# SyncE takes over the stores of the w1/w2 products and the loads of their blocks

## Chip, cores and metric

One core of a Trainium2 chip. The metric is the device time of one execution in microseconds (us). The engines are TensorE (PE; PEld is its weight load), VectorE (DVE), ScalarE (ACT), GpSimd (POOL) and SyncE (SP). A name with a q (SPq, ACTq) is the engine's sequencer, which waits, branches and issues DMAs.

## The reference, cut to what matters

Input x is 4 sequences x 2048 rows x 256 columns, float32. Two blocks follow each other, each with a residual and a layernorm:

```python
x = layernorm(x + mamba(x))        # 256 -> 512 channels, 16 states, a scan over 2048 rows
h = silu(x @ w1 * s1) * (x @ w2 * s2)          # 256 -> 1024, ternary weights
h = gelu(h @ h1 * sh1); h = gelu(h @ h2 * sh2) # 1024 -> 1024
x = layernorm(x + h @ w3 * s3)                 # 1024 -> 256
```

In the Mamba block, for each channel d and state n: `h = exp(delta * A) * h + (delta * u) * B`, `y = sum over n of h * C`.

## The kernel before, in words

The program has two stages. The first (lines 198 to 1400) holds the Mamba block and, woven into it, the products with w1 and w2; it leaves the first block's rows in x1 and the products in the DRAM tensor ab. The second (`split_stage`, from line 1425) reads ab back and does the rest of the FFN, bound by matmuls; nothing in it is touched.

**Tiles, chunks, groups, slots.** The first stage goes over 16 tiles of 512 rows (4 sequences x 4). A tile has 4 chunks of 128 channels (c = 0 to 3), a chunk 16 groups, a group 128 lanes (32 channels x 4 states) x 512 rows. Each group needs one decay on ACT (`decay_of`, line 908, `exp(delta * A)`), one scan on VectorE (`scan`, line 1267), part of a product with B (VectorE line 1251 for three of four steps, POOL line 1129 for the fourth) and part of a product with C (POOL line 1118). TensorE sums the latter over the states (`fold_step`, line 650).

**Order by hand.** Each engine's program of the first stage is unrolled over the 64 slots of a tile, i = 0 to 63; in slot i VectorE scans group 20 + i (the numbering runs into the next tile), ACT computes the decay of two groups later (`EXP_LEAD`), and the tables at the top (`DT_SLOTS`, `AB_PLACES`, ...) say in which slot every other piece of work stands. There are three decay banks and three places for h. Twelve tiles run in a hardware loop, four tiles a turn; the last four are written out.

**The w1/w2 products.** A tile has 16 of them (e = 0 to 15), 128 x 512 float32 each, in the slots of `AB_PLACES`. TensorE multiplies in slot s (`ffn_product`, line 722), ACT copies the bank to one of three buffers in slot s + 1 (`copy_product`, line 972) and stores the buffer to ab in slot s + 2 (`ffn_stores`, `store`, line 957). The copy waits until its buffer is free, that is until the store of product e - 3 has landed:

```python
act.wait_ge(ab_out[e % ABRING], t.count(ab_uses(e), 16 * (e // ABRING) + ABOUT0))
```

Product 6's matmuls wait for copy 5 (same bank), the step sizes of the next tile's chunk 1 for copy 6, those of chunk 2 for copy 14. The weights come in 8 blocks of 256 KB (one for two products) into four places; behind every second copy ACT issues the load of the block four further on (`load_w12`, line 951).

**SP's program** (lines 418 to 535). For each chunk `copies(t, c)` does four things: it writes delta to DRAM when POOL has it (line 422), writes delta * u (line 424), waits until that has landed and loads it back four times, spread over the lanes (du_bc, line 432, 4 DMAs), and does the same with delta (d_bc, line 439, 4 DMAs). Between the chunks' copies stand the store of x1 (line 456), the load of x into the same buffer (line 485, behind the landing of that store) and the load of the next xT (line 415). SP is not written by slots: it runs through this list and each item waits for its semaphores. In the last tile it also loads what the FFN's first layer of a later stage needs (`closing_loads`, `closing`, lines 498 to 525).

Of the kernel before, what the change touches and what calls it, by code (L numbers as in the profile page):

```python
# [14 lines left out]
P = 128  # L15
# [3 lines left out]
NT = 512  # L19
# [56 lines left out]
def is_first(t):  # L76
    return t.number() == 0
# [33 lines left out]
LN_SLOT = 15  # L111
EXP_LEAD = 2


XT_PLACES = ((16, 2), (18, 1))
AB_PLACES = ((23, 0), (25, 0), (28, 2), (30, 2), (32, 2), (34, 2), (36, 2), (38, 1), (40, 1), (41, 0), (44, 2), (46, 2),
# [12 lines left out]

ROUND_SLOTS = (8, 12, 16, 20, 24, 28, 32, 36)  # L130
RAW_PLACES = 2
GATE_SLOT, FIRST_SLOT = 42, 51
FIRST_BANKS = (5, 6, 7, 3)
EARLY_POOL_PIECES = 4
PAST_BANKS = (0, 4, 2, 1)
# [59 lines left out]
def mamba_stage(nc, sems, flag, xT, x, in_wT, conv_w, conv_b, xp_wT, dt_wT, dt_b, A_log, D_param, out_wT,  # L195
                fold, spread, ident, w1T, w2T, h1T, h2T, w3T, scales, d_rows, du_rows, w12, x1, ab):
    ctx = ExitStack()
    with ctx:
# [185 lines left out]

        kept.stores += [(ab_out[k], PAST.count(ab_uses(k), ab_uses(k) + ABOUT0)) for k in range(ABRING)]

        block = ctx.enter_context(nc.Block())

        WEIGHTS = 12
# [7 lines left out]
        def _(sp):  # L397
# [17 lines left out]
                sp.dma_start(xT_sb[:], xT[t.b, :, t.tt * NT:(t.tt + 1) * NT]  # L415
                             .rearrange("(k p) t -> p k t", p=P)).then_inc(xT_in, 16)

            def copies(t, c):

                k = c % 2  # L420
                sp.wait_ge(delta, t.count(KI, c + 1))
                sp.dma_start(d_rows[k], sp_r[k][:]).then_inc(d_out[k], 16)
                sp.wait_ge(du, t.count(KI, c + 1))
                sp.dma_start(du_rows[k], sp_w[k][:]).then_inc(du_out[k], 16)

                sp.wait_ge(db_dve, t.count(KI * QV, QV * (c - 1) + DVE0))
                sp.sem_inc(waited, 1)
                sp.wait_ge(db_pool, t.count(KI, c - 1 + POOL0))
                sp.sem_inc(waited, 1)
                sp.wait_ge(du_out[k], t.count(32, 16 * (c // 2 + 1)))  # L430
                for nn in range(GN):
                    sp.dma_start(du_bc[k][nn * GD:(nn + 1) * GD, :, :],
                                 du_rows[k].rearrange("(j d) t -> d j t", d=GD)).then_inc(du_in[k], 16)

                sp.wait_ge(decay, t.count(NG, GC * (c - 1) + DECAY0))
                sp.sem_inc(waited, 1)
                sp.wait_ge(d_out[k], t.count(32, 16 * (c // 2 + 1)))
                for nn in range(GN):
                    sp.dma_start(d_bc[k][nn * GD:(nn + 1) * GD, :, :],
                                 d_rows[k].rearrange("(j d) t -> d j t", d=GD)).then_inc(d_in[k], 16)  # L440

            def load_next(t):

# [21 lines left out]
                load_piece(sp, open_raw[j][:], j).then_inc(open_in[j], 16)  # L465

            sp.wait_ge(checked, 8)
            copies(OPENING, 0)
            load_next(OPENING)
            copies(OPENING, 1)  # L470
            copies(OPENING, 2)

            def tile(t):
                nxt = t.following()
                rows = slice(t.tt * NT, (t.tt + 1) * NT)
                if t is LAST_ROW[-1]:
                    closing_loads(t)
                copies(t, 3)
                store_x1(t)
# [5 lines left out]
                sp.dma_start(res[:], x[t.b, rows, :].rearrange("(s p) c -> p s c", p=P)).then_inc(x_in, 16)  # L485
                if exists(nxt):
                    copies(nxt, 0)
                if exists(nxt.following()):
                    load_next(nxt)
                if exists(nxt):  # L490
                    copies(nxt, 1)
                    copies(nxt, 2)

            def load_pool(j):
                if j >= RAW_PLACES:
# [13 lines left out]
            def closing(t):  # L509
                for m in range(KH):  # L510
# [9 lines left out]
                sp.wait_ge(first_lo, KH)  # L520
                for j in range(RAW_PLACES + EARLY_POOL_PIECES):
                    load_pool(j)
                store_x1(PAST)
                for j in range(RAW_PLACES + EARLY_POOL_PIECES, H2_PIECES + W3_PIECES):
                    load_pool(j)
# [3 lines left out]
                    tile(SeqTile(b, tt))  # L529
            for t in LAST_ROW:  # L530
                tile(t)
            closing(LAST_ROW[-1])
            sp.wait_ge(x1_out, PAST.count(16, 16))

        @block.tensor
# [269 lines left out]
        def _(act):  # L805
# [141 lines left out]
                                  x_t[k][:].bitcast(F32).rearrange("p a t -> p (a t)").rearrange("p (m c) -> p m c", c=P)  # L947
                                  ).then_inc(w12_out, 16)

            def load_w12(t, m):  # L950
                act.dma_start(w12_sb[m % W12RING][:].bitcast(F32), w12[m]).then_inc(w12_in[m % W12RING], 16)

            def store(t, e):
                at = (ab[0:TILES].rearrange("(b q) e p t -> b q e p t", q=TILES_B)[t.b, t.tt, e] if exists(t)
                      else ab[TILES, e])
                act.wait_ge(ab_sb, ab_done(t, e + 1))
                act.dma_start(at, ab_sbuf[e % ABRING][:]).then_inc(ab_out[e % ABRING], 16)

            def transposed(t, k, step):
                src = bank[XT_PLACES[k][1]]  # L960
                if step == 1:
# [30 lines left out]
            def closing_pass(t, i):  # L992

# [38 lines left out]
                act.activation(mid[0][:, m, :], hring[m % len(hring)][:], ACT.Copy).then_inc(mid_hi, 1)  # L1032

            def closing():
                ffn_stores(PAST, 0)
# [21 lines left out]
            def tile(t):  # L1057
                nxt = t.following()
                for i in range(NG):
                    n = OFF + i  # L1060
                    if t is BEFORE and i in W12_SLOTS:
                        round_w12(W12_SLOTS.index(i))
                    if t is BEFORE and i == W12_FIRST:
                        act.wait_ge(w12_out, 16 * 2 * KM)
                        for m in range(W12RING):
                            load_w12(OPENING, m)
                    if exists(t):
                        ffn_stores(t, i)
# [23 lines left out]
                if exists(t):  # L1092
                    ffn_stores(t, NG)

            tile(BEFORE)
            with act.Fori(0, BATCH - 1) as b:
# [1010 lines left out]
```

## Time and profile before

| | |
|---|---|
| median of 3 runs | 3103.6 us (3101.23 to 3104.07) |
| the profiled execution, its own time | 3103.3 us |
| its span in the profile | 3101.5 us |
| VectorE, POOL, TensorE, ACT busy, share of the span | 75%, 58%, 88%, 65% |
| the first stage | to some 2034 us |
| SP's queue (q1), ACT's queue (q10) | 297.67 MB, 112.22 MB |

Busy times are those of the engines' own instructions; issuing a DMA is not counted. A line of the timeline gives start, duration, engine and line, what is written and read, and how many instructions were merged (x4); in brackets stands the idle time before it and what ended it. "Landing" is the time from the issue of a DMA to its semaphore.

### The profile page before, as it was taken

Reading aid. Unit: us, or ns where it says so; the run is one execution under the profiler, and the core shown is the slowest. Engines: PE = TensorE matmul, PEld = TensorE weight load, DVE = VectorE, ACT = ScalarE, POOL = GpSimd, SP = SyncE. Lnnn points to the kernel's source line nnn. Section 1 sums busy time; section 2 is a strip of 40 time slices with the busy share of each in tenths; the row PEclk is TensorE's granted clock in tenths of the full one; section 3 lists DMA queues with packets and bytes.
Section 4 is the critical chain, followed back from the end, with each engine's and each line's share of the span. In section 5 each row is a group of like instructions: output and inputs, shape, how many; then the busy total and the mean of one; then the engine's idle time right before and its main releaser. Section 6 shows DMA issues by size and latency. Waiting matters only on the chain. (4 is left out here: it accounts for less than half of the span.)

```text
span 3101.5 us, 39954 instructions
## 1 busy us (share of the span) xinstructions
PE 2724.2 (88%) x11028; PEld 1636.8 (53%) x11028; DVE 2338.7 (75%) x2781; ACT 2010.8 (65%) x3383; POOL 1784.3 (58%) x920
## 2 busy tenths in 40 slices
PE   5788988888888888888888876889999999999997
PEld 2243443343343333333333332678888888888886
DVE  5999999999999999999999999434444454444442
ACT  3777777777777777777777777555555445555442
POOL 3899999899899899999999999400000000000000
PEclk8888898989889889889889887899999999999999
DMA  7366466466475475564565566542222222222210
GB/s 254 93 189 166 121 192 163 117 190 164 118 194 149 131 197 134 145 195 127 155 183 130 164 166 192 199 159 87 83 68 88 74 68 87 89 68 83 80 41 15
DMA packets 239642, 411.98 MB, mean 133 GB/s; under 512 B 23264, under 2 KB 63456, under 8 KB 239456
## 3 DMA queue, kind: packets, MB, share of 16 engines
q1 hardware_dynamic: 175680, 297.67, 35.3%
q10 hardware_dynamic: 63776, 112.22, 11.2%
q8 instruction: 69, 1.13, 0.2%
q14 instruction: 117, 0.96, 0.1%
HBM read 285.55 MB, written 124.26 MB: 132 GB/s over the span
## 5 line engine op out<-in xcount | busy, mean ns | idle before, releaser
L1267 DVE TENSOR_TENSOR_SCAN h<-bank,state,db 128x512 f32<-128x512 f32 x1024 | 1252.5, 1266 | 70.9 <-ACT bank L908 37.5
L1118 POOL TENSOR_TENSOR hc<-h,c_rows 128x1024 f32<-128x1024 f32 x512 | 1202.0, 2378 | 15.3 <-DVE h L1267 10.4
L908 ACT ACTIVATE bank<-d_bc,a_neg 128x512 f32<-128x512 f32 x1024 | 692.8, 685 | 314.5 <-DVE h L1267 201.9
L1627 ACT ACTIVATE hring<-s_bank,sc 128x512 f32<-128x512 f32 x248 | 170.5, 688 | 488.9 <-PE s_bank L1560 488.5
L1560 PE MATMUL s_bank<-mid,h_r 128*128 128x512 f32 x2048 | 469.1, 390 | 4.6 <-DVEq L1654 4.6
L722 PE MATMUL bank<-x_t,w 128*128 128x512 f32 x1088 | 394.1, 492 | 55.8 <-ACT ab L972 46.9
L1251 DVE TENSOR_TENSOR db<-bank,du_bc 128x2048 f32<-128x2048 f32 x192 | 435.1, 2266 | 8.1 <-issue 7.8
L1560 PEld LDWEIGHTS s_bank<-mid,h_r 128*128 128x128 f32 x2048 | 385.8, 188 | 85.6 <-ACTq L1598 5.0
L1129 POOL TENSOR_TENSOR db<-du_bc,b_row 128x2048 f32<-128x2048 f32 x64 | 291.7, 4558 | 102.4 <-DVE h L1267 97.7
L629 PE MATMUL bank<-bc,w_spread 64*128 64x512 f32 x272 | 155.6, 581 | 217.7 <-DVE db L1251 214.5
L650 PE MATMUL bank<-hc,fold_w 128*32 128x512 f32 x2048 | 334.6, 731 | 8.6 <-DVE u L1291 5.0
L722 PEld LDWEIGHTS bank<-x_t,w 128*128 128x128 f32 x1088 | 220.4, 217 | 215.4 <-issue 102.7
L629 PEld LDWEIGHTS bank<-bc,w_spread 64*128 64x128 f32 x272 | 58.0, 215 | 396.4 <-DVE db L1251 275.8
L582 PE MATMUL bank<-xb,w_conv 128*128 128x512 f32 x512 | 254.2, 626 | 13.4 <-ACT uz L829 9.5
L972 ACT ACTIVATE ab<-bank 128x512 f32<-128x512 f32 x272 | 160.1, 588 | 122.3 <-PE bank L722 107.7
L1560 PE MATMUL s_bank<-s_end,h_r 128*128 128x512 f32 x1024 | 235.7, 391 | 0.0
L1685 DVE TENSOR_TENSOR mid<-hring,mid 128x512 fp32r<-128x512 f32 x120 | 81.5, 690 | 177.7 <-ACT mid L1630 177.7
L1560 PEld LDWEIGHTS s_bank<-s_end,h_r 128*128 128x128 f32 x1024 | 191.8, 188 | 41.4
L582 PEld LDWEIGHTS bank<-xb,w_conv 128*128 128x128 f32 x512 | 90.0, 192 | 162.8 <-issue 142.9
L1560 PE MATMUL s_bank<-first_lo,h_r 128*128 128x512 f32 x448 | 175.4, 391 | 0.0
L1560 PE MATMUL s_bank<-first_hi,h_r 128*128 128x512 f32 x448 | 175.3, 391 | 0.0
L1685 DVE TENSOR_TENSOR first_lo<-hring,first_hi 128x512 fp32r<-128x512 f32 x64 | 44.3, 692 | 147.3 <-ACT first_hi L1630 147.3
(143 smaller groups left out, 3698.1 us busy)
## 6 DMA issues: line engine op xcount, KB each, us to landing
ab<-ab ACTq DMA_DIRECT2D x272, 256.0 KB, 4.1
du_bc<-du_rows SPq DMA_DIRECT2D x256, 256.0 KB, 4.9
d_bc<-d_rows SPq DMA_DIRECT2D x256, 256.0 KB, 7.9
s_abr<-ab SPq DMA_DIRECT2D x120, 512.0 KB, 3.9
w<-w ACTq DMA_DIRECT2D x136, 256.0 KB, 3.9
d_rows<-sp_r SPq DMA_DIRECT2D x64, 256.0 KB, 2.0
du_rows<-sp_w SPq DMA_DIRECT2D x64, 256.0 KB, 2.0
x<-res SPq DMA_DIRECT2D x17, 512.0 KB, 8.9
```

The costliest lines, as they stand in the source:

```text
L582: last = pe.matmul(p_mm[j % 2][:], w_conv[:, c, k, :], xb[:, c, k:k + NT], start=k == 0, stop=k == TAPS - 1)
L629: pe.matmul(dst[:], spread_w[:, which, :], bc[t.tt % 2][DTR:P, :], start=True, stop=True).then_inc(done, 1)
L650: last = pe.matmul(p_y[GD * j:GD * j + GD, :], fold_w[:], hc[:, k % HCSTEPS, j, :], start=q == 0, stop=q == QN - 1, tile_position=(0, GD * j))
L722: last = pe.matmul(product_bank(t, e)[:], w12_sb[m % W12RING][:, which, k, :], x_t[j][:, k, :], start=k == 0 and j == 0, stop=k == KM - 1 ...
L908: act.activation(decays[DECAY_BANK[g]][:], d_bc[c % 2][:, j, :], ACT.Exp, scale=a_neg[:, g:g + 1]).then_inc(decay, 1)
L972: act.activation(ab_sbuf[e % ABRING][:], product_bank(t, e)[:], ACT.Copy, scale=-1.0).then_inc(ab_sb, 1)
L1118: pool.tensor_tensor(hc[:, k % HCSTEPS, at:at + HG], h[:, H_SLOT[k], at:at + HG], c_rows[:, q, :].unsqueeze(1).broadcast_to([P, HG, NT]), ...
L1129: pool.tensor_tensor(db[:, k % DBSTEPS], du_bc[c % 2][:], b_row[:].unsqueeze(1).broadcast_to([P, JC, NT]), ALU.mult).then_inc(db_pool, 1)
L1251: dve.tensor_tensor(db[:, k % DBSTEPS], p_b[:].unsqueeze(1).broadcast_to([P, JC, NT]), du_bc[c % 2][:], ALU.mult).then_inc(db_dve, 1)
L1267: dve.tensor_tensor_scan(h[:, H_SLOT[k], j, :], decays[DECAY_BANK[g]][:], db[:, k % DBSTEPS, j, :], state[:, g:g + 1], ALU.mult, ALU.add). ...
L1560: last = pe.matmul(p_h[m % HBANKS][:], hidden_weights(layer, k, m), ins[j][:, k, :], start=k == 0 and j == 0, stop=k == KH - 1 and j == pa ...
L1627: act.activation(hring[c % RING][:], p_h[m % HBANKS][:], ACT.Gelu, scale=sc[:, 2 + layer, m:m + 1]).then_inc(gelu, 1)
```

## The change

The stores of the products and the loads of the w1/w2 blocks of the 16 tiles are issued by SP; those of the closing stay with ACT, the load now behind the store. For that SP's program is written by slots as the others are: `copies` is cut into four steps in the slots 6 to 9 behind a chunk's `DT_SLOTS`, so in slots 26 to 29 (next tile's chunk 0), 44 to 47 (chunk 1), 60 to 63 (chunk 2) and 12 to 15 (this tile's chunk 3). The store of product e stands in slot `AB_PLACES[e][0] + 2`, as on ACT before, ahead of that slot's copies step; behind an odd one stands the block's load. x1 is stored in slot 17, x loaded in slot 23, xT in slot 34. In the last tile the first layer's loads and the first two pieces of h2 get slots too.

```diff
+COPY_AFTER, COPY_STEPS = 6, 4
+STORE_SLOT, X_SLOT, XT_SLOT = 17, 23, 34
...
-GATE_SLOT, FIRST_SLOT = 42, 51
+FIRST_LOADS = {25: (0, 1), 29: (2, 3, 4, 5), 38: (6, 7)}
+GATE_SLOT, FIRST_SLOT, POOL_LOAD_SLOT = 42, 51, 56
...
+        def load_w12(eng, t, m):
+            if m >= W12RING or not is_first(t):
+
+                eng.wait_ge(ab_sb, ab_done(t, 2 * (m - W12RING) + 2))
+            eng.dma_start(w12_sb[m % W12RING][:].bitcast(F32), w12[m]).then_inc(w12_in[m % W12RING], 16)
+
+        def store(eng, t, e):
...
+            eng.wait_ge(ab_sb, ab_done(t, e + 1))
+            eng.dma_start(at, ab_sbuf[e % ABRING][:]).then_inc(ab_out[e % ABRING], 16)
...
-            def copies(t, c):
+            def copies(t, c, step):
...
+                if step == 0:
+                    sp.wait_ge(delta, t.count(KI, c + 1))
+                    sp.dma_start(d_rows[k], sp_r[k][:]).then_inc(d_out[k], 16)
+                elif step == 1:
+                    sp.wait_ge(du, t.count(KI, c + 1))
+                    sp.dma_start(du_rows[k], sp_w[k][:]).then_inc(du_out[k], 16)
+                elif step == 2:
...
+            def products(t, i):
+
+                for e in range(AB):
+                    if i == AB_PLACES[e][0] + 2:
+                        store(sp, t, e)
+
+                        m = e // 2 + W12RING
+                        if e % 2 == 1 and m < KH:
+                            load_w12(sp, t, m)
+                        elif e % 2 == 1 and exists(t):
+                            load_w12(sp, t.following(), m - KH)
...
+                for i in range(NG):
+                    if t is LAST_ROW[-1]:
+                        first_loads(t, i)
+                    products(t, i)
+                    for step in range(COPY_STEPS):
+                        for now, c in dt_places(t, i, COPY_AFTER + step):
+                            if exists(now):
+                                copies(now, c, step)
+                    if i == STORE_SLOT:
+                        store_x1(t)
+                    elif i == X_SLOT:
+                        load_x(t)
+                    elif i == XT_SLOT and exists(nxt.following()):
+                        load_next(nxt)
...
-            def load_w12(t, m):
-                act.dma_start(w12_sb[m % W12RING][:].bitcast(F32), w12[m]).then_inc(w12_in[m % W12RING], 16)
-
-            def store(t, e):
...
-                act.wait_ge(ab_sb, ab_done(t, e + 1))
-                act.dma_start(at, ab_sbuf[e % ABRING][:]).then_inc(ab_out[e % ABRING], 16)
...
-                m = e // 2 + W12RING
-                if e % 2 == 1 and m < KH:
-                    load_w12(t, m)
-                elif e % 2 == 1 and exists(t):
-                    load_w12(t.following(), m - KH)
...
-            def ffn_stores(t, i):
-                for e in range(AB):
-                    if i == AB_PLACES[e][0] + 2:
-                        store(t, e)
...
-                    store(PAST, e)
+                    store(act, PAST, e)
+                    m = e // 2 + W12RING
+                    if e % 2 == 1 and m < KH:
+                        load_w12(act, PAST, m)
```

## Rows read from the trace of the kernel before

**Rows 1.** Busy time by window: window, its length, each engine's busy us, clock, DMA

```profile
82.00:1954.00 1872.00, 1578.32 (x5652) 694.92 (x5652) 1790.17 (x1545) 1402.28 (x2481) 1730.91 (x873) 0.88 0.58 159
```

**Rows 2.** VectorE's waits, 80 to 1954 us: us in total, times, longest

```profile
DVE h L1267 <- ACT bank L908: 37.5, 49, 2.9
DVE h L1267 <- POOL hc L1118: 29.4, 19, 2.0
DVE bank L1274 <- ACT bank L881: 6.3, 25, 0.9
```

**Rows 3.** ACT's groups by line: busy us, mean ns, idle before and its releasers

```profile
L908 ACT ACTIVATE bank<-d_bc,a_neg 128x512 f32<-128x512 f32 x1024 | 692.8, 685 | 314.5 <-DVE h L1267 201.9 <-ACT ab L972 87.0 <-DMA d_bc<-d_rows 21.5
```

**Rows 4.** ACT's timeline, tile 0: store 2, then copy 5, its store, decays

```profile
170.82 0.36 ACTq L957 DMA_DIRECT2D ab<-ab  x1
...
180.87 0.59 ACT L972 ACTIVATE ab<-bank 128x512 f32<-128x512 f32 x1
181.62 0.34 ACTq L957 DMA_DIRECT2D ab<-ab  x1
182.07 1.30 ACT L908 ACTIVATE bank<-d_bc,a_neg 128x512 f32<-128x512 f32 x2 [0.62 <-ACT ab L972]
```

**Rows 5.** VectorE's timeline behind a tile's last product (tile 3)

```profile
583.76 1.28 DVE L1267 TENSOR_TENSOR_SCAN h<-bank,state,db 128x512 f32<-128x512 f32 x1 [0.75 <-ACT bank L908]
```

**Rows 6.** SP's timeline, tile 0: the loads of du_bc, chunks 0 and 1

```profile
173.62 1.74 SPq L432 DMA_DIRECT2D du_bc<-du_rows  x4
...
205.46 1.84 SPq L432 DMA_DIRECT2D du_bc<-du_rows  x4
```

**Rows 7.** SP's timeline, tile 3: chunk 3's first loads and x1's store

```profile
500.21 1.75 SPq L432 DMA_DIRECT2D du_bc<-du_rows  x4
...
504.15 0.41 SPq L456 DMA_DIRECT2D x<-res  x1
```

**Rows 8.** Line 439, the last two d_bc loads of that chunk, and their landing

```profile
L439 SPq DMA_DIRECT2D d_bc<-d_rows x2: 432/432/432, 503.0 to 503.4; - x2
...
DMA to landing us min/median/max: 7.8/8.1/8.4
```

**Rows 9.** DMA issues, 80 to 1954 us: count, KB each, median us to landing

```profile
d_bc<-d_rows SPq DMA_DIRECT2D x252, 256.0 KB, 7.9
ab<-ab ACTq DMA_DIRECT2D x249, 256.0 KB, 4.3
...
x<-res SPq DMA_DIRECT2D x16, 512.0 KB, 8.9
```

**Rows 10.** ACT's timeline, tile 3: store 3 and copy 6

```profile
526.54 0.34 ACTq L957 DMA_DIRECT2D ab<-ab  x1
...
535.57 0.60 ACT L972 ACTIVATE ab<-bank 128x512 f32<-128x512 f32 x1 [1.20 <-DMA ab<-ab]
```

**Rows 11.** VectorE's timeline, tile 0: slots 36 to 39, slot 40, slot 56

```profile
181.20 4.80 DVE L1267 TENSOR_TENSOR_SCAN h<-bank,state,db 128x512 f32<-128x512 f32 x4
187.78 1.28 DVE L1267 TENSOR_TENSOR_SCAN h<-bank,state,db 128x512 f32<-128x512 f32 x1 [1.78 <-POOL hc L1118]
...
216.87 1.28 DVE L1267 TENSOR_TENSOR_SCAN h<-bank,state,db 128x512 f32<-128x512 f32 x1 [0.74 <-ACT bank L908]
```

**Rows 12.** TensorE's timeline: product 6 of tile 0, a product of tile 15

```profile
181.51 1.19 PE L722 MATMUL bank<-x_t,w 128*128 128x512 f32 x4 [1.09 <-ACT ab L972]
...
1936.83 2.05 PE L722 MATMUL bank<-x_t,w 128*128 128x512 f32 x4 [0.78 <-ACT ab L972]
```

**Rows 13.** SP's timeline, tile 14: the loads of du_bc, chunks 0 and 1

```profile
1819.35 1.77 SPq L432 DMA_DIRECT2D du_bc<-du_rows  x4
...
1852.09 1.79 SPq L432 DMA_DIRECT2D du_bc<-du_rows  x4
```

**Rows 14.** VectorE's timeline, tile 14: slot 40; slots 55 and 56

```profile
1834.69 1.28 DVE L1267 TENSOR_TENSOR_SCAN h<-bank,state,db 128x512 f32<-128x512 f32 x1 [1.77 <-POOL hc L1118]
...
1861.10 2.43 DVE L1267 TENSOR_TENSOR_SCAN h<-bank,state,db 128x512 f32<-128x512 f32 x2
```

More of the change, by code:

```diff
@@ L385, in mamba_stage @@
         kept.stores += [(ab_out[k], PAST.count(ab_uses(k), ab_uses(k) + ABOUT0)) for k in range(ABRING)]
+        def load_w12(eng, t, m):
[3 more added lines that the diff above has]
+        def store(eng, t, e):
+            at = (ab[0:TILES].rearrange("(b q) e p t -> b q e p t", q=TILES_B)[t.b, t.tt, e] if exists(t)
+                  else ab[TILES, e])
+            eng.wait_ge(ab_sb, ab_done(t, e + 1))
+            eng.dma_start(at, ab_sbuf[e % ABRING][:]).then_inc(ab_out[e % ABRING], 16)
         block = ctx.enter_context(nc.Block())
@@ L416, in load_xT @@
                              .rearrange("(k p) t -> p k t", p=P)).then_inc(xT_in, 16)
-            def copies(t, c):
+            def copies(t, c, step):
                 k = c % 2
[L421 to L440, printed above, removed]
@@ new lines, in copies @@
+                if step == 0:
[5 more added lines that the diff above has]
+                elif step == 2:
+                    sp.wait_ge(db_dve, t.count(KI * QV, QV * (c - 1) + DVE0))
+                    sp.sem_inc(waited, 1)
+                    sp.wait_ge(db_pool, t.count(KI, c - 1 + POOL0))
+                    sp.sem_inc(waited, 1)
+                    sp.wait_ge(du_out[k], t.count(32, 16 * (c // 2 + 1)))
+                    for nn in range(GN):
+                        sp.dma_start(du_bc[k][nn * GD:(nn + 1) * GD, :, :],
+                                     du_rows[k].rearrange("(j d) t -> d j t", d=GD)).then_inc(du_in[k], 16)
+                else:
+                    sp.wait_ge(decay, t.count(NG, GC * (c - 1) + DECAY0))
+                    sp.sem_inc(waited, 1)
+                    sp.wait_ge(d_out[k], t.count(32, 16 * (c // 2 + 1)))
+                    for nn in range(GN):
+                        sp.dma_start(d_bc[k][nn * GD:(nn + 1) * GD, :, :],
+                                     d_rows[k].rearrange("(j d) t -> d j t", d=GD)).then_inc(d_in[k], 16)
@@ L467, in _, with load_x @@
             sp.wait_ge(checked, 8)
[L468 to L479, printed above, removed]
+            for c in range(KI - 1):
+                for step in range(COPY_STEPS):
+                    copies(OPENING, c, step)
+                if c == 0:
+                    load_next(OPENING)
+            def load_x(t):
                 sp.wait_ge(x1_out, t.count(16, 16))
@@ L484, in tile @@
                 sp.sem_inc(waited, 1)
[L485 to L492, printed above, removed]
+                sp.dma_start(res[:], x[t.b, t.tt * NT:(t.tt + 1) * NT, :].rearrange("(s p) c -> p s c", p=P))\
+                  .then_inc(x_in, 16)
+            def tile(t):
+                nxt = t.following()
+                if t is LAST_ROW[-1]:
+                    closing_loads(t)
+                for i in range(NG):
+                    if t is LAST_ROW[-1]:
+                        first_loads(t, i)
+                    products(t, i)
+                    for step in range(COPY_STEPS):
+                        for now, c in dt_places(t, i, COPY_AFTER + step):
[7 more added lines that the diff above has]
+                        load_next(nxt)
             def load_pool(j):
@@ L507, in closing_loads, with first_loads @@
                     load_piece(sp, raw[j][:], j).then_inc(raw_h1_in[j], 16)
-            def closing(t):
-                for m in range(KH):
+            def first_loads(t, i):
+                for m in FIRST_LOADS.get(i, ()):
                     if m == 2:
@@ L519, in closing @@
                       .then_inc(first_in[m // (KH // 2)], 16)
-                sp.wait_ge(first_lo, KH)
-                for j in range(RAW_PLACES + EARLY_POOL_PIECES):
+                if i == POOL_LOAD_SLOT:
+                    sp.wait_ge(first_lo, KH)
+                    for j in range(RAW_PLACES):
+                        load_pool(j)
+            def closing():
+                for j in range(RAW_PLACES, RAW_PLACES + EARLY_POOL_PIECES):
                     load_pool(j)
@@ L531, in _ @@
                 tile(t)
-            closing(LAST_ROW[-1])
+            closing()
             sp.wait_ge(x1_out, PAST.count(16, 16))
@@ L948, in round_w12 @@
                                   ).then_inc(w12_out, 16)
-            def load_w12(t, m):
-                act.dma_start(w12_sb[m % W12RING][:].bitcast(F32), w12[m]).then_inc(w12_in[m % W12RING], 16)
-            def store(t, e):
-                at = (ab[0:TILES].rearrange("(b q) e p t -> b q e p t", q=TILES_B)[t.b, t.tt, e] if exists(t)
-                      else ab[TILES, e])
-                act.wait_ge(ab_sb, ab_done(t, e + 1))
-                act.dma_start(at, ab_sbuf[e % ABRING][:]).then_inc(ab_out[e % ABRING], 16)
             def transposed(t, k, step):
@@ L1034, in closing @@
             def closing():
-                ffn_stores(PAST, 0)
                 norm(PAST, LN_SLOT - 8)
@@ L1065, in tile @@
                         for m in range(W12RING):
-                            load_w12(OPENING, m)
-                    if exists(t):
-                        ffn_stores(t, i)
+                            load_w12(act, OPENING, m)
                     now, g = at_group(t, n + EXP_LEAD)
@@ L1091, in tile @@
                         closing_pass(t, i)
-                if exists(t):
-                    ffn_stores(t, NG)
             tile(BEFORE)
```

## The prediction

> **What bounds the kernel now.** First the window of the recurrence, 82 to 1954 us [rows 1]: VectorE is busy 1790 of its 1872 us, POOL 1731, TensorE 1578, ACT 1402. The second stage keeps its program and its loads, so what the change is worth is what it does to the 82 us in which VectorE stands still in the first. The list of VectorE's waits [rows 2] says who ends them: ACT's decays (line 908) 37.5 us, POOL's products 29.4 us, ACT's logarithm (line 881) 6.3 us. ACT's group of decays [rows 3] shows why ACT can be late with a quarter of its time free: the decays waited 87.0 us in all for line 972, the copy of a product. The reader is to see in ACT's timeline [rows 4] what that wait is: copy 5 of tile 0 starts at 180.87 and ends at 181.46, the store is issued at 181.62 and the decay starts at 182.07, 0.62 us behind the copy's end. The store waits on ACT for ACT's own copy, and all that is behind it in ACT's program waits with it. The load of a w1/w2 block waits for nothing and is issued while ACT still computes: no idle time of ACT stands behind it.
>
> A slot is the time of one scan; a tile has 64, and 15 tiles have a next tile whose chunks SP spreads.
>
> **The change part by part.**
>
> *Taken from ACT.* 16 stores a tile, each with 0.62 us on ACT's path, and 8 loads at 0. This reaches the end only where VectorE waits for ACT: at least 0, at most 37.5 + 6.3 = 44 us. Where do those waits stand? Many are near slots 40 to 58, where the next part puts a later wait over them. One is away from it: product 15's store is the last thing ahead of the SiLU of z, and VectorE then waits 0.75 us for a decay [rows 5]. I take one store, 0.6 us, times 15 tiles: 9 us of gain.
>
> *Added to SP.* 24 DMA issues a tile of 0.34 us [rows 4] are 8 us of a tile's 117 (1872 / 16); SP's chunk copies wait for POOL in any case, so this costs nothing by itself. What counts is the order. SP's program is in order, and so is its queue. Store 2 stands at slot 30, behind all four steps of the next tile's chunk 0 (slots 26 to 29), among them eight DMAs of 256 KB, du_bc and d_bc: the block. Store 11 stands at slot 48, behind those of chunk 1 (44 to 47). Now they leave 2.8 us ahead of the block (170.82 against 173.62 [rows 4, 6]), or with it.
>
> *When does a store behind the block land?* The x1 store is such a DMA: on the same queue, right behind the block of chunk 3, with nothing on ACT's queue. The block's first du_bc is issued at 500.21 [rows 7]; the later of its last two d_bc is issued at 503.4 and lands 8.4 us later [rows 8], at 511.8, which is 11.6 us from the first du_bc. The x1 store, issued at 504.15 [rows 7], lands after 8.9 us [rows 9], at 513.05: 1.2 us behind the last d_bc, for 512 KB. A product's 256 KB take half, 0.6 (an estimate). So stores 2 and 11 land 11.6 + 0.6 = 12.2 us after the block's first du_bc; 12.3 with the wake-up of the one who waits. Even on its own queue a store issued into the block is no faster: the one of 526.54 held copy 6 back until 535.57, 9.0 us, and ACT stood 1.20 us for it [rows 10].
>
> *Who waits.* There are three buffers, so copy 5 (slot 35) waits for store 2, and copy 14 (slot 53) for store 11. Both stand in ACT's program ahead of the decay for the scan three slots later. In tile 0 copy 5 ran at 180.87; now it can't before 173.62 + 12.3 = 185.9, 5 us late. Then 0.58 (copy) and 0.67 (decay): slot 38's scan starts 1.25 us later, at 187.2, and with two scans of 1.18 us slot 40's starts at 173.62 + 12.3 + 3.6 = 189.5. It started at 187.78 [rows 11]. The difference is 1.7 us and not 5, since ACT was ahead, and since POOL stopped VectorE there for 1.78 us anyway: that wait covers part of the new one. Copy 6 has a product before it that needs copy 5's bank; with 1.19 us of matmuls [rows 12] it is done just in time for slot 40. Copy 14: 205.46 + 12.3 + 1.25 = 219.0 against slot 56 at 216.87 [rows 6, 11], 2.1 us. Tile 0 loses 3.9 us. Tile 14, the last of the 15, by the same sum [rows 13, 14]: 1819.35 + 15.9 = 1835.3 against 1834.69, 0.6; 1852.09 + 13.55 = 1865.6 against 1862.3 (the second of the two scans from 1861.10), 3.4; together 4.0. With the others like these, 15 x 3.9 = 58 us. A stall shifts POOL and the next chunk's delta with it, so nothing later makes up for it.
>
> *Bounds.* If the last d_bc lands 0.5 us sooner (the median over all blocks is 7.9 [rows 9]), each of the 30 stalls is 0.5 shorter: 58 - 15 = 43. If a block takes 1 us longer, as its queue now also holds two stores and two w1/w2 loads (0.6 each, most of them ahead of its start), 30 more: 88. I take 58, by the block that stood alone in its time, as these will.
>
> *The rest.* x1's store and x's load at slots 17 and 23 keep their neighbours: 0. The xT load goes at slot 34, and its reader is 13 slots away: 0. Stores 0, 1, 3 and 4 and the w1/w2 blocks have 6 to 16 slots until someone needs them: 0, covered as long as the queue is empty again by slot 40. The earlier loads of the last tile wait for the same semaphores as before: 0. In the closing, where ACT still stores, a w1/w2 load now follows its store: 4 x 0.34 us where ACT has gaps, 0 to 1.4, taken as 0.
>
> **Sum.** 58 - 9 = +49 us on the profiled execution's own 3103.3 us: 3152. The median of the runs is 3103.6, 0.3 above, which changes nothing. A difference under 0.2% (6 us) can't be told from none here.
>
> By the Trainium skill (DMA: Bandwidth & Descriptors, Issuing engines are not separate DMA queues) DMAs of all issuing engines share the same 16 DMA engines, and spreading the issues saves sequencer time alone. By that rule alone the move costs nothing and ACT's time is gained, as in A below. The same page (Queues, rings and completion order) gives SP and ACT a ring each, drained in order; the x1 store of rows 7 and 9 is on the side of this second rule.
>
> **Rivals.**
> *A, faster.* The stores are not held up by the block. Place: copies 5 and 14. It decides whether a store lands within 8.7 us of the first du_bc (slot 38's scan starts at 181.20 + 2.36 = 183.6 [rows 11]; less 1.25, less 173.62), not 12.3. For it: the stores' median landing is 4.3 us [rows 9]. Against: rows 7 to 10. Then 9 to 44 us are gained, about the middle, 25: 3078. Chance 0.15, of it 0.02 within 0.2%.
> *B, half of it.* VectorE's waits for POOL (29.4 us) shrink as each new stall lets POOL catch up, and they take half of the 58: 3103 + 29 - 9 = 3123. For it: POOL's waits stand beside the new ones. Against: slot 40's is counted already. Chance 0.17, of it 0.03 within 0.2%.
> *C, more than the sum.* TensorE is held too: the product behind copy 5 and the step-size product behind copy 14 wait, and ACT waits for both. Four matmuls took 2.05 us at the lower clock, 1.19 at the higher [rows 12]; 0.86 at each of the two places and tile, 15 x 1.7 = 26 us: 3178. Chance 0.08.
> *D, nothing.* Neither the late stores nor ACT's gain reach VectorE: 3103. Against: copy 5 has under 3 us to spare. Chance 0.02.
> *My forecast* has 0.58; its own range is 3128 (3103 + 43, less 18, twice the gain taken) to 3182 (3103 + 88 - 9).
>
> **How the numbers follow.** Faster: A, 0.13. Within 0.2%: 0.02 + 0.03 + 0.02 = 0.07. Slower: 0.14 + 0.58 + 0.08 = 0.80. The range goes from 3095 (most of A left out) to 3183 (C in).
>
> **What the changed profile would show.** Decays back to back with the copies, no longer 0.62 us behind. Copies 5 and 14 each waiting 2 to 5 us for the DMA of a product, stores 2 and 11 landing some 9 us after their issue; line 972's waits for that DMA up by 70 us or more in all. VectorE's waits for ACT's decays up from 37.5 to some 90, most of them at slots 38 and 56. If ACT's wait for stores stays near what it was and VectorE's for ACT falls, the step "a store behind the block lands at 12.2 us" was wrong, and A holds. If copies 5 and 14 wait as said and VectorE's waits grow by less than 30 us, B holds.

## The result, and the profile after

| | before | after |
|---|---|---|
| median of the runs, us | 3103.8 (3101.2 to 3104.4, 4 runs) | 3250.7 (3231.1 to 3269.5, 4 runs) |
| profiled execution, us | 3103.3 | 3269.5 |
| its span, us | 3101.5 | 3267.4 |

The ratio is 1.047 (95% interval 1.041 to 1.054): the kernel is 147 us slower, where the forecast was 49 and the range ended at 80 above. The profiled execution is the slowest of the four, 19 us above their median; sums over its trace are held against its own 166 us.

The window of the recurrence is 164 us longer (82 to 2118 instead of 82 to 1954), so nothing of the loss lies outside it. Busy time by window (window, length, busy us of PE, PEld, DVE, ACT, POOL, then the granted clock, the DMA share and GB/s), against [rows 1]:

```profile
82.00:2118.00 2036.00, 1641.58 (x5648) 724.12 (x5648) 1789.21 (x1545) 1388.07 (x2478) 1728.77 (x873) 0.84 0.55 146
```

VectorE and POOL do what they did (1789 and 1729 us). TensorE is busy 63 us longer at a lower granted clock. The time went into waits: VectorE stands still 247 us of the window, not 82. Who ends those waits (us in total, times, longest; line 1291 is the scan, line 1298 a step of delta), against [rows 2]:

```profile
DVE h L1291 <- ACT bank L954: 229.2, 96, 6.9
DVE bank L1298 <- ACT bank L927: 14.5, 15, 1.0
```

ACT's decays went from 37.5 to 229.2, and the 29.4 us of waits for POOL are gone. What ACT itself waits for, in the same stretch (line 1009 is the copy of a product, line 954 the decay, line 912 the first step of softplus, line 965 the residual):

```profile
ACT ab L1009 <- DMA ab<-ab: 205.8, 32, 7.6
ACT bank L954 <- DVE h L1291: 166.9, 220, 2.6
ACT ab L1009 <- PE bank L768: 129.4, 123, 4.0
ACT sp_e L912 <- PE bank L660: 40.5, 17, 2.8
ACT res L965 <- PE bank L717: 40.3, 26, 3.3
```

Assigned to products, the 205.8 us are copy 5 with 107.0 (16 times), copy 14 with 93.8 (15 times) and copy 3 once with 5.0: but for that one, the two places of the forecast. Before, only copy 6 waited for a store, 9.6 us in all. DMA issues over the whole program (KB each, median us to landing):

```profile
du_bc<-du_rows SPq DMA_DIRECT2D x256, 256.0 KB, 4.7
d_bc<-d_rows SPq DMA_DIRECT2D x256, 256.0 KB, 7.7
ab<-ab SPq DMA_DIRECT2D x256, 256.0 KB, 3.2
```

The median store lands sooner than before (3.2 us, 4.3 in [rows 9]); a median doesn't show the two in sixteen that matter. One of those, store 2, is in the timelines of tile 8 (tiles are counted from 0), SP first:

```profile
1190.01 0.34 SPq L439 DMA_DIRECT2D d_rows<-sp_r  x1
1190.60 0.34 SPq L401 DMA_DIRECT2D ab<-ab  x1
1190.99 0.45 SPq L395 DMA_DIRECT2D w<-w  x1
1191.49 0.43 SPq L442 DMA_DIRECT2D du_rows<-sp_w  x1
1194.60 1.74 SPq L451 DMA_DIRECT2D du_bc<-du_rows  x4
1196.53 1.73 SPq L459 DMA_DIRECT2D d_bc<-d_rows  x4
1198.52 0.97 SPq L401 DMA_DIRECT2D ab<-ab  x2
```

then ACT and VectorE:

```profile
1199.38 0.69 ACT L954 ACTIVATE bank<-d_bc,a_neg 128x512 f32<-128x512 f32 x1
1207.12 0.60 ACT L1009 ACTIVATE ab<-bank 128x512 f32<-128x512 f32 x1 [7.05 <-DMA ab<-ab]
1207.61 1.29 ACT L954 ACTIVATE bank<-d_bc,a_neg 128x512 f32<-128x512 f32 x2
...
1214.47 0.69 ACT L912 ACTIVATE sp_e<-bank,dtb 128x512 f32<-128x512 f32 x1 [2.72 <-PE bank L660]
```

```profile
1208.42 2.46 DVE L1291 TENSOR_TENSOR_SCAN h<-bank,state,db 128x512 f32<-128x512 f32 x2 [4.89 <-ACT bank L954]
1211.44 1.28 DVE L1291 TENSOR_TENSOR_SCAN h<-bank,state,db 128x512 f32<-128x512 f32 x1 [0.56 <-ACT bank L954]
...
1217.85 1.28 DVE L1291 TENSOR_TENSOR_SCAN h<-bank,state,db 128x512 f32<-128x512 f32 x1 [1.76 <-ACT bank L954]
```

Store 2 is issued at 1198.52, directly behind the block. Copy 5 starts at 1207.12, 12.5 us behind the first du_bc, and the scan of slot 38 1.30 us later, after VectorE stood 4.89 us. So far this is the forecast's own chain. The rest is on TensorE, then on POOL:

```profile
1198.09 1.06 PE L696 MATMUL bank<-hc,fold_w 128*32 128x512 f32 x8
1199.08 1.19 PE L768 MATMUL bank<-x_t,w 128*128 128x512 f32 x4
1207.77 2.08 PE L768 MATMUL bank<-x_t,w 128*128 128x512 f32 x4 [7.49 <-ACT ab L1009]
1209.77 0.79 PE L675 MATMUL bank<-bc,w_spread 64*128 64x512 f32 x1
1210.50 1.93 PE L696 MATMUL bank<-hc,fold_w 128*32 128x512 f32 x8
1212.36 2.07 PE L660 MATMUL bank<-xd,w_dt 64*128 64x512 f32 x2
```

```profile
1224.06 4.74 POOL L1142 TENSOR_TENSOR hc<-h,c_rows 128x1024 f32<-128x1024 f32 x2 [6.76 <-PE bank L696]
1228.74 1.28 POOL L1161 TENSOR_TENSOR sp_r<-sp_r,sp_e 128x512 f32<-128x512 f32 x1
```

TensorE stands idle 7.49 us for the bank that copy 5 should empty. The windows ahead of, in and behind that wait (busy us of PE, PEld, DVE, ACT, POOL, then the granted clock):

```profile
1192.00:1200.00 8.00, 8.00 (x36) 3.77 (x28) 8.00 (x7) 5.97 (x11) 8.00 (x4) 1.00 0.84 198
1200.00:1207.70 7.70, 0.28 (x2) 0.00 (x0) 3.53 (x4) 0.65 (x3) 7.70 (x4) 0.72 1.06 254
1207.70:1214.40 6.70, 6.63 (x16) 2.18 (x16) 5.42 (x4) 3.12 (x7) 5.16 (x3) 0.50 0.60 229
1214.40:1224.00 9.60, 8.83 (x23) 4.13 (x23) 6.89 (x8) 7.09 (x13) 2.90 (x2) 0.51 0.29 95
```

The granted clock falls from 1.00 (2.4 GHz) to 0.50 (1.2 GHz) over the wait and stays there while the work that had piled up is done. Four matmuls of a product take 2.08 us, 1.19 ahead of the wait; a fold (line 696) 1.93 and 1.06; the spreading (line 675) 0.79, where 0.50 is usual in the trace of before; the step-size product (line 660) 2.07, where the same two matmuls took 1.12 there. Together that is 3.0 us more. ACT's softplus waits 2.72 us for the last of them, and VectorE 1.76 us for ACT. POOL, which needs the folds' bank, stands 6.76 us, and the delta of the next chunk (line 1161) comes late with it. POOL's waits for folds were 2.6 us in all before:

```profile
POOL hc L1142 <- PE bank L696: 182.8, 43, 7.1
```

**Where each microsecond is.** From the start of every scan, the time from one slot to the next, mean of the 15 tiles, after less before, times 15. A plus is time lost; only slots with over 1.5 us are named.

| step | us | what ends it |
|---|---|---|
| slot 38 | +74.5 | copy 5 late |
| slot 40 | -19.3 | POOL's wait there, now covered |
| slot 42 | +24.5 | softplus behind the slow step-size product |
| slot 43 | +11.9 | softplus behind the held TensorE |
| slot 56 | +74.5 | copy 14 late |
| slot 64 | +11.9 | work behind store 11 (below) |
| slots 2, 52, 54, 59 | -16.6 | stores off ACT, short waits covered |

The named ones give 161.4; the whole is 160.4 (15 tiles took 1921.3 us, 1760.9 before).

**Two tiles in which the clock came back.** The tiles aren't alike, and that tells a late store from a slow TensorE. In tiles 1 and 4 copy 5 is late too: slot 38 loses 3.8 and 4.9 us, in the other 13 tiles 3.2 to 6.2. But there the granted clock is back at 1.00 before the step-size product. TensorE and POOL in tile 1:

```profile
314.92 2.08 PE L768 MATMUL bank<-x_t,w 128*128 128x512 f32 x4 [5.92 <-ACT ab L1009]
317.64 1.86 PE L696 MATMUL bank<-hc,fold_w 128*32 128x512 f32 x8
319.44 1.12 PE L660 MATMUL bank<-xd,w_dt 64*128 64x512 f32 x2
```

```profile
331.06 1.28 POOL L1161 TENSOR_TENSOR sp_r<-sp_r,sp_e 128x512 f32<-128x512 f32 x1
```

and the windows from product 6 to the fold's end and over the step-size product:

```profile
314.80:319.40 4.60, 4.48 (x13) 1.65 (x13) 3.28 (x3) 3.17 (x7) 4.47 (x3) 0.51 0.82 308
319.40:320.60 1.20, 1.20 (x7) 0.41 (x4) 1.20 (x2) 0.00 (x1) 0.89 (x1) 1.00 0.04 12
```

The table gives the loss against the same tile of the kernel before, as a mean per tile in us. The delta is that of chunk 1, behind slot 44 (5.6 to 6.6 us before).

| | tiles 1 and 4 | the other 13 |
|---|---|---|
| granted clock, slots 38 to 41 | 0.71 | 0.50 |
| slot 38 | 4.4 | 5.1 |
| slot 42 | 0.0 | 1.9 |
| delta (not a loss) | 4.6 | 6.3 to 7.9 |
| slot 56 | 1.7 | 5.5 |
| slot 64 | -0.3 | 1.0 |
| slots 37 to 64 together | 4.5 | 11.8 |

So the late stores alone cost some 4.5 us a tile, near the forecast's 3.9, and the low clock behind them another 7.3 us in 13 tiles, 95 us (an estimate, as no run sets the clock). The length of the stall doesn't sort the tiles: tile 14 has the shortest (3.2 us), keeps 0.50 and loses 12.3.

### The profile page after: what moved, and what is told of

Its sections match the earlier page's. It is cut to its first block and busy times, and to the rows that moved or that the text cites. A ratio compares the mean times of both kernels' runs of the same rounds, so it can differ in the third digit from the quotient of the medians.

```text
span 3267.4 us, 40072 instructions
## 1 busy us (share of the span) xinstructions
PE 2788.9 (85%) x11028; PEld 1666.8 (51%) x11028; DVE 2338.0 (72%) x2781; ACT 1997.6 (61%) x3383; POOL 1781.6 (55%) x920
## 5 line engine op out<-in xcount | busy, mean ns | idle before, releaser
L1291 DVE TENSOR_TENSOR_SCAN h<-bank,state,db 128x512 f32<-128x512 f32 x1024 | 1255.9, 1271 | 231.0 <-ACT bank L954 229.2
L1142 POOL TENSOR_TENSOR hc<-h,c_rows 128x1024 f32<-128x1024 f32 x512 | 1199.9, 2371 | 197.6 <-PE bank L696 182.8
L768 PE MATMUL bank<-x_t,w 128*128 128x512 f32 x1088 | 412.3, 511 | 149.5 <-ACT ab L1009 139.2
L768 PEld LDWEIGHTS bank<-x_t,w 128*128 128x128 f32 x1088 | 229.8, 226 | 320.9 <-issue 138.3
L1009 ACT ACTIVATE ab<-bank 128x512 f32<-128x512 f32 x272 | 161.4, 594 | 346.4 <-DMA ab<-ab 205.8
L660 PE MATMUL bank<-xd,w_dt 64*128 64x512 f32 x128 | 96.3, 842 | 64.6 <-ACT ab L1009 55.0
```

The source lines that it names most:

```text
L768: last = pe.matmul(product_bank(t, e)[:], w12_sb[m % W12RING][:, which, k, :], x_t[j][:, k, :], start=k == 0 and j == 0, stop=k == KM - 1 ...
L1142: pool.tensor_tensor(hc[:, k % HCSTEPS, at:at + HG], h[:, H_SLOT[k], at:at + HG], c_rows[:, q, :].unsqueeze(1).broadcast_to([P, HG, NT]), ...
L1291: dve.tensor_tensor_scan(h[:, H_SLOT[k], j, :], decays[DECAY_BANK[g]][:], db[:, k % DBSTEPS, j, :], state[:, g:g + 1], ALU.mult, ALU.add). ...
```

## The experiments

All of them change the kernel after, and all keep the whole computation. Each was timed beside the kernel before on one chip, so the ratios to that kernel are the comparison. Positions below are medians over tiles 1 to 14, in us behind the start of slot 26 (chunk 0) or 44 (chunk 1). "Block" is again the eight loads of du_bc and d_bc.

**Who issues what.** The w1/w2 loads go back to ScalarE, which issues them behind its copies; the stores stay. (The lines that ScalarE gets aren't shown.)

```
-                        if e % 2 == 1 and m < KH:
-                            load_w12(sp, t, m)
-                        elif e % 2 == 1 and exists(t):
-                            load_w12(sp, t.following(), m - KH)
```

> The changed kernel (3250.7 us), with the loads of the w1/w2 blocks issued by ACT again; SP keeps the stores. Order theory (the loss comes from stores 2 and 11, which now wait behind the block of du_bc and d_bc loads): both stores stay behind the block, so nearly all of the loss stays. One load fewer stands ahead of du_rows in the queue, so the block starts some 0.6 us earlier, 9 us in all, and what follows from it: 3225 to 3245. Queue theory (one queue carries too much; each DMA moved to it costs its share): 8 of 24 moved DMAs go back, a third of the loss with them: about 3200.

Measured: 3269.9 us, ratio 1.054 (1.048 to 1.060), so neither number. The interval overlaps that of the kernel after: it is not faster, and not shown to be slower. Chunk 0's block did start earlier (8.7 us, after 10.5), but it took longer, 12.7 us from first du_bc to last d_bc landed instead of 11.7, and chunk 1's 12.9 instead of 11.9. The store landed 13.2 and 13.8 us behind the first du_bc. What no longer stands ahead of the block now runs beside it, on the other queue, and makes it longer.

Now the reverse: stores back on ScalarE in the same slots, loads on SyncE.

```
-                        store(sp, t, e)
+            def ffn_stores(t, i):
+                for e in range(AB):
+                    if i == AB_PLACES[e][0] + 2:
+                        store(act, t, e)
...
+                    if exists(t):
+                        ffn_stores(t, i)
```

> The changed kernel with the stores of the products issued by ACT again, in the slots of before; SP keeps the slots and the loads of the w1/w2 blocks. Order theory: copies 5 and 14 no longer wait for stores behind the block, and the whole loss is gone: 3098 to 3110; ACT's wait of the copy line for a store's DMA falls from 205.8 us to under 20. Queue theory: the loads still crowd SP's queue, a third of the loss stays: about 3150. Slot theory (the new order of SP's own program, its x, xT and x1 items, costs time): 3150 or more.

Measured: 3105.1 us, ratio 1.001 (1.000 to 1.002). The eight loads on SyncE's queue and its program written by slots cost nothing; the whole loss comes from the stores. ScalarE issues store 2 1.8 us ahead of the block's first load; in the kernel after SyncE, which first waits until du_rows has landed and then issues the eight loads, comes to it 3.9 us behind. VectorE's waits are back at those of [rows 2]:

```profile
DVE h L1296 <- ACT bank L952: 38.2, 49, 2.0
DVE h L1296 <- POOL hc L1147: 28.6, 19, 2.0
```

**The order alone.** Everything stays on SyncE; the chunk-copy steps of chunks 0 and 1 move two slots later, behind stores 2 and 11.

```
-COPY_AFTER, COPY_STEPS = 6, 4
+COPY_AFTER, COPY_STEPS = (8, 8, 6, 6), 4
...
```

> The changed kernel with the four copy steps of the next tile's chunks 0 and 1 two slots later (offsets 8 to 11 instead of 6 to 9), so that stores 2 and 11 stand ahead of the du_bc and d_bc loads in SP's program. All else is as in the changed kernel: SP issues every store and load. Order theory: the loss is gone and ACT's saving stays: 3075 to 3105; VectorE's wait for ACT's decays under 40 us. Queue theory: the same DMAs in the same queue cost the same: above 3220.

Measured: 3087.7 us, ratio 0.995 (0.993 to 0.997). This separates order from engine and from load: the same DMAs on the same queue, 163 us apart. Store 2 lands 0.65 us behind the first du_bc instead of 12.44, store 11 0.89. ACT's waits for a store's DMA are now mostly copy 6's, 39.4 us in 15 tiles (store 3 stands behind the block instead), with 10.4 us of copies 3, 5 and 9 in four places. Hardly any of it reaches VectorE (slot 40 loses 1.8 us in all):

```profile
ACT ab L1010 <- DMA ab<-ab: 49.8, 19, 5.3
```
```profile
DVE h L1292 <- ACT bank L955: 25.7, 35, 2.6
...
DVE h L1292 <- POOL hc L1143: 19.5, 11, 2.0
```

**The two stores of the forecast.** Stores 2 and 11 on ScalarE, the other fourteen on SyncE; then the same with `(11,)`, so that only store 2 is late, and with `(2,)`.

```
+ACT_STORES = (2, 11)
...
-                        store(sp, t, e)
+                        if e not in ACT_STORES:
+                            store(sp, t, e)
+                    for e in ACT_STORES:
+                        if exists(t) and i == AB_PLACES[e][0] + 2:
+                            store(act, t, e)
```

> The changed kernel with two of a tile's sixteen stores, those of products 2 and 11, issued by ACT again; the other 14 stores and the 8 loads stay with SP. Order theory: these two make the loss, so the time comes back to 3095 to 3125 (copy 6 then has to wait a little for store 3, which stays behind the block). Queue theory: two of 24 DMAs are an eighth of the stores' part at most: above 3220.

Measured: 3105.7 us, ratio 1.0006 (0.9994 to 1.0017). Taking two of sixteen stores off SyncE takes the whole loss away. But a third one shows up: copy 6 waits 60.5 us for store 3, also behind the block. Slot 40 loses 15.0 us to it, and chunk 1's delta comes 7.35 us behind slot 44 instead of 5.89, nearly as late as in the kernel after (7.51).

> The changed kernel with store 11 issued by ACT; store 2 stays behind the block. Follow-on theory (the part of the loss that the prediction missed comes from store 2: copy 5 late holds product 6 on TensorE, that holds the folds and POOL, and so chunk 1's delta, and copies 6 and 7): slots 38 to 43 keep their +92 us (net), chunk 1's delta stays some 7.5 us behind slot 44 (5.9 in the kernel before), slot 56 is free: 3150 to 3175. Rival (two stalls a tile feed each other over SP's queue; one alone costs what the prediction's sum gave, 23 us): 3115 to 3125, slot 42 free.

Measured with only store 2 late: 3165.7 us, ratio 1.020 (1.018 to 1.023), 63 us. The larger ones by slot: 38 +77.4, 40 -19.3, 42 +20.7, 43 +11.1, 56 -10.0. The sum came as expected and slot 56 is free, so the stall at 38 needs no second late store to cost the 32 us of slots 42 and 43. The delta was a miss: 6.6 us behind slot 44, not 7.5. Here four tiles (1, 3, 11 and 13) have the clock back before the step-size product, with the delta at 4.6 and nothing lost at slot 42; each of the other eleven loses 1.8 to 2.0 us there.

> The changed kernel with store 2 issued by ACT; store 11 stays behind the block. Follow-on theory: chunk 1's delta is back at 5.9 us behind slot 44, so slot 56 costs some 45 us instead of 74.5 (1.6 + 0.3 us less in 15 tiles), slots 38 to 43 are free but for copy 6's wait: 3120 to 3145. Rival (delta is late from something else in SP's new order): slot 56 keeps its 74.5, 3160 or more.

Measured with only store 11 late: 3195.9 us, ratio 1.030 (1.027 to 1.033), 93 us, the rival's number. Slot 56 loses 71.7, not the 45 expected: chunk 1's block still starts late (10.3 us), because copy 6's wait for store 3 is there (63.9 us) and holds TensorE and the delta (6.8 us). Slot 40 adds 19.5 from it, slot 43 8.1. Slot 64 loses 9.1, and with only store 2 late it gained 4.6, so its loss belongs to store 11. The two single losses add up to 156 us against 147 together, but that doesn't show the two stalls to be independent: copy 6's wait, which the kernel after doesn't have, stands in for copy 5's and delays the delta in its place.

**What moves the blocks.** The order experiment, with the block's two halves spread further: du_bc at offset 10, d_bc at 12, for chunks 0 and 1.

```
-COPY_AFTER, COPY_STEPS = 6, 4
+COPY_STEPS = 4
+COPY_AFTER = ((6, 7, 10, 12), (6, 7, 10, 12), (6, 7, 8, 9), (6, 7, 8, 9))
...
```

> The changed kernel with the copy steps of chunks 0 and 1 at offsets 6, 7, 10 and 12: delta and delta * u are written as early as in the changed kernel, du_bc is loaded behind store 2 (11) and d_bc behind store 3 (12). Order theory: copy 6, which waited 39 us for store 3 with the steps two slots later, waits under 15 us; no store is behind a whole block: 3075 to 3090, at or a little under the kernel with the steps two slots later (3087.7). Rival (what copy 6 waits for is hidden behind POOL at slot 40 anyway, and later loads of d_bc hold the decays of the next chunk): 3090 to 3105.

Measured: 3085.3 us, ratio 0.995 (0.993 to 0.997). Copy 6 waits 1.2 us in all, and chunk 1's delta is at 5.91 us, where it was before. Over the runs, copy 6's waits of 60.5, 39.4 and 1.2 us go with deltas at 7.35, 6.16 and 5.91, and with 41.8, 14.5 and 5.3 us of waits of POOL for folds: a copy that waits delays the next chunk's delta through TensorE's folds and POOL, even where hardly a scan waits for that copy.

Then the kernel after with one pair swapped: in slot 27 du_rows of chunk 0 goes ahead of store 1 and the w1/w2 load behind it.

```
-                    products(t, i)
+                    if i != 27:
+                        products(t, i)
...
+                    if i == 27:
+                        products(t, i)
```

> The changed kernel with one pair swapped: in slot 27 the write of du_rows (chunk 0) stands ahead of store 1 and the w1/w2 load behind it in SyncE's program. Theory, queue ahead of the block: in the changed kernel du_rows of chunk 0 lands 3.4 us after its issue (2.3 before), because 512 KB of store and load stand ahead of it, and the block starts 10.5 us after slot 26 (9.2 before). With the swap the block starts at 9.3 to 9.8, store 2 still lands 12.4 us behind its start, slot 37 to 38 gives 0.7 to 1.2 us a tile back: 3233 to 3242 against 3250.7. Rival, load of the queue: store 1 and its load now run beside du_rows and into the block, which gets longer by as much as it starts earlier (as it did with the loads on ScalarE's queue, 12.7 against 11.7), and nothing is gained: 3248 to 3256.

Measured: 3230.7 us, ratio 1.043 (1.039 to 1.046). Its interval overlaps that of the kernel after, so the 20 us are likely and not proven. What the trace does show is that the block of chunk 0 starts at 9.2 us, as before the change, and that slot 38 loses 61.7 us instead of 74.5. The rest of the gain is not the swap's own: in this execution six tiles, not two, have the clock back in time, and they lose 4.3 us each in slots 37 to 64, the other nine 10.6. SP's timeline of the swapped kernel:

```profile
1175.34 0.33 SPq L442 DMA_DIRECT2D du_rows<-sp_w  x1
1175.90 0.34 SPq L401 DMA_DIRECT2D ab<-ab  x1
1176.30 0.45 SPq L395 DMA_DIRECT2D w<-w  x1
1177.39 1.74 SPq L451 DMA_DIRECT2D du_bc<-du_rows  x4
```

From du_rows to du_bc it is 2.05 us; in the kernel after, with a store and a load ahead in the queue, 3.11 (1191.49 to 1194.60). Half of the gain is paid back inside the block (12.2 us, 11.7 after), as the rival had it.

**Is there a better version?** First the kernel after with the five stores that stand behind a block (2, 3, 4, 11, 12) on ScalarE, by the same lines as above.

> The changed kernel with stores 2, 3, 4, 11 and 12, those that stand behind a block, issued by ScalarE; the other eleven and all w1/w2 loads stay with SyncE. Theory, order: with stores 2 and 11 alone on ScalarE copy 6 still waited 60.5 us for store 3, the next chunk's delta came 1.5 us late for it, and the time was 3105.7. Now no copy waits for a store's DMA by more than 5 us in all, chunk 1's delta is back at 5.9 us after slot 44, and 11 of 16 stores cost ScalarE nothing: 3085 to 3098, below the kernel before. Rival, load of the queue: eleven stores and the loads on SyncE's queue make the blocks late by themselves, stalls stay at slots 38 and 56: 3105 to 3125.

Measured: 3086.4 us, ratio 0.9955 (0.9942 to 0.9968). No copy waits over 6 us in all for a store, and POOL's waits for folds, 182.8 us after and 41.8 with two stores on ScalarE, are down to 3.9 (us, times, longest):

```profile
POOL hc L1147 <- PE bank L698: 3.9, 15, 0.5
```

Second, the spread kernel with chunk 0's d_bc at offset 14, behind store 4 (`(6, 7, 10, 14)`).

> The kernel with the copy steps spread (offsets 6, 7, 10, 12), changed once more: chunk 0's d_bc step moves to offset 14, behind store 4. There copy 7 waited 35.6 us for store 4, which stood behind d_bc. Theory, order: that wait goes, and with it what it cost: 3078 to 3085 against 3085.3. Rival, the wait was hidden: 3085 to 3088. Third way: d_bc of chunk 0 now lands too late for the first decay of the next tile's chunk (some 2 slots less room); then VectorE's wait for ScalarE's decays grows at slots 41 to 43 and the time is 3090 or more.

Measured: 3085.4 us, ratio 0.995 (0.993 to 0.997). Copy 7's 35.6 us of waiting are gone and the time stays: that wait was hidden. Four ways to keep late stores out of the way, these two and the two shifts of the order, end at 3085 to 3088, 14 to 17 us below the kernel before beside them; their intervals overlap, so none is shown to be the best.

A fourth and fifth buffer for the copies, which should take the wait away as well, wasn't tried. That stays open.

## Why the prediction was wrong in size

*The place and the first link were right.* Stores 2 and 11 behind the block, copies 5 and 14 waiting for them, slots 38 and 56. The term "a store behind the block lands at 12.2 us" measured 12.44, and 12.52 with the wake-up against 12.3. Copy and decay took 1.30 at slot 38 against 1.25, 1.48 at slot 56. Each wait was longer than the 2 to 5 us named, 6.7 us for copy 5 and 6.3 for copy 14 in the mean. Moving the order alone takes the loss away (0.995), moving two stores does too (1.0006).

*The step that failed* is that the sum takes TensorE at the higher clock behind the wait and lets it delay nothing: "with 1.19 us of matmuls [rows 12] it is done just in time for slot 40", and "A stall shifts POOL and the next chunk's delta with it, so nothing later makes up for it", which makes a stall cost its own length and no more. Product 6 took 2.08 us at the clock of 0.50, and what stood behind it was slowed as well. Slots 42 and 43 lost 36 us, slot 64 lost 12, and chunk 1's delta came later against slot 44 than before, by 1.1 us in the mean of the 15 tiles, which is 17 of the 74.5 at slot 56. Where the clock was back in time (tiles 1 and 4), the whole loss was 4.5 us a tile, near the 3.9 of the sum; in the other 13 it was 11.8.

*Rival C named this and undersized it.* "TensorE is held too" was priced at 0.86 us at each place for four slower matmuls, 26 us, with a chance of 0.08. But everything that stood behind the held product ran at the lower clock: the fold, the spreading and the step-size product, 3.0 us in tile 8, enough for ACT's 2.72 us of waiting. Slot 43 is the exception: it loses 0.8 us in tiles 1 and 4 as in the others. How much of that is the hold itself and how much the clock until it came back stays open.

*A second step failed*, worth less: "Stores 0, 1, 3 and 4 and the w1/w2 blocks have 6 to 16 slots until someone needs them: 0", and with it the start of the block, taken unchanged from the trace of before. It moved at both places (medians, us):

| | before | after | why |
|---|---|---|---|
| chunk 0's first du_bc, behind slot 26 | 9.23 | 10.50 | store 1 and a load ahead of du_rows |
| chunk 1's first du_bc, behind slot 44 | 9.27 | 11.11 | delta 5.89 to 7.51 |
| slot 26 to 38 | 19.17 | 24.31 | |
| slot 44 to 56 | 20.91 | 25.26 | |

The forecast's sum on these medians is 9.23 + 12.3 + 1.25 = 22.8, a loss of 3.6 at slot 38, and 22.8 less 20.91 = 1.9 at slot 56. Measured are 5.1 and 4.35. Of the 1.5 missing at slot 38 the start of the block has 1.3, of the 2.4 at slot 56 1.8. I looked for who waits for a store and not for what stands behind it in the queue: with 512 KB ahead of it du_rows took 3.4 us to land instead of 2.0. That is chunk 0's part, 1.3 us in 15 tiles, some 20 us; chunk 1's part is the late delta above. The price was in "If a block takes 1 us longer", but as something that fell "most of them ahead of its start" and hence was left out of the sum.

*POOL's wait.* The 1.78 us that POOL would stop VectorE anyway at slot 40 covered 1.29 us a tile (19.3 / 15), so 7 us less than taken.

*The gain* was taken as 9 us, one store's 0.6 in 15 tiles behind product 15. Measured are 16.6 in short waits at four slots. At the place named (slot 64) the kernel after loses 11.9 and gains nothing; with five stores on ScalarE, where product 15's store is still SyncE's, the same slot gains 4.6.

*Summed up:* forecast 58 - 9 = 49. Measured in the profiled execution, 74.5 + 74.5 - 19.3 = 130 in place of 58, another 48 in slots 42, 43 and 64 in place of 0, less 17.

*Rival A*, no loss, fell at the number set for it: copies 5 and 14 could start 12.5 us behind the block's first load, not 8.7. The rule of the Trainium skill that stood beside it (DMA: Bandwidth & Descriptors, Issuing engines are not separate DMA queues), that the issuing engine saves sequencer time alone, doesn't agree with these runs: the same stores in the same slots issued by ScalarE instead of SyncE are 1.001, against 1.047. What it leaves out is when a DMA gets issued: SyncE's program stood waiting ahead of store 2. That all DMAs share the same engines does agree: with the w1/w2 loads on the other queue the block took 1 us longer. Its other section (Queues, rings and completion order) says that each DMA engine takes turns between the queues for which it has work, packet by packet. These runs neither bear that out nor rule it out. In the kernel before store 11, issued on ScalarE's queue together with the block's first load, landed after 4.0 us, while the block took 14.1. But stores 3 and 12, issued on that queue 2.0 and 3.0 us into a block, took 7.9 and 8.6, about as long as stores 2 and 11 on SyncE's queue behind the block, 8.5 and 8.4 from their own issue. So the recorded remark that a store issued into the block is no faster on its own queue holds, within these few tenths.

*Rival B* had POOL's waits take back half of the loss. They did shrink to nothing (29.4 us), but slot 40's 19.3 are nearly all that this gave, against some 197 lost at the other slots.

## What to carry to other kernels

When DMAs move to another engine, list that engine's program in order and read two things: who waits for the moved one behind a large block, and what small, urgent one now stands behind the moved one. Then follow a stall past the engine it was priced for. A copy out of a TensorE bank that waits for a buffer holds TensorE, and what TensorE then runs late, it ran slowly here (its granted clock was 0.50 behind the wait); that made two stalls a tile cost 11.8 us in 13 tiles, and 4.5 in the two where the clock was back. With the order right, the engine that issues hardly matters: 3085 to 3088 us with all stores on SyncE or with five on ScalarE.

## What the runs showed of the hardware

The same eight 256 KB loads, issued in one go, took 11.7 to 11.9 us with nothing on the other queue (the kernel after), 12.1 to 12.9 with only stores or only loads there (both experiments on who issues what), and 13.4 to 14.1 with both (the kernel before). So the block was never shorter with a second queue in use. Nor was a second queue by itself a way past the block: what counted was whether the store was issued ahead of it or with its first load (it landed after 2.1 us as store 2 and 4.0 as store 11 in the kernel before) or 2 to 7 us into it (7 to 10 us on either queue). A single 256 KB store behind the block added 0.8 us to it (12.44 less 11.66, where the last d_bc had landed), near the 0.6 worked out from x1's store.
